# Counting sort of the edges: one-hots, histograms and lookups as engine loops of four groups instead of written out

## The reference

```python
h = x @ Wn.T + bn;  e = edge_attr @ We.T + be
a = leaky_relu(sum((h[src] + e) * attn), 0.01)
a = softmax of a over the edges that share dst
x = layernorm(x + relu(segment_sum(h[src] * a, dst)))      # first layer
agg = segment_sum(x[src'], dst');  cnt = segment_sum(1, dst')
x = layernorm(x + x @ W1.T + b1 + (agg / max(cnt, 1)) @ W2.T + b2)
```

## Time and profile before

| | |
|---|---|
| time before, median of 3 runs | 1555.24 us (1553.36 to 1556.54) |
| profiled execution | 1551.7 us, span of the core 1548.2 us |
| granted TensorE clock, mean | 0.904 |
| TensorE busy | 1198.5 us, 77% of the span |
| VectorE busy | 1067.6 us, 69% |
| ScalarE busy | 767.5 us, 50% |
| GpSimd busy | 746.3 us, 48% |

### The profile page before, as it was taken

One profiled execution on the slowest core, in us unless ns is written; L12 is line 12 of the kernel. 1 busy time (PEld: TensorE's weight loads), 2 busy tenths in 40 slices (PEclk: granted clock), 3 DMA queues, 4 the chain that ended last, 5 costly groups with the idle time before them and its releaser, 6 DMA issues.

```text
span 1548.2 us, 24971 instructions
## 1 busy us (share of the span) xinstructions
PE 1198.5 (77%) x6537; PEld 1030.5 (67%) x6537; DVE 1067.6 (69%) x4021; ACT 767.5 (50%) x1718; POOL 746.3 (48%) x731
## 2 busy tenths in 40 slices
PE   4567667627602999994999999998996888888884
PEld 3456556626501888883888888787785777777773
DVE  8855567515568555553999999998898666666661
ACT  5543357314300444442777777676775344434442
POOL 1066660466660677775444410555533345655563
PEclk9898889969955999997999999999999888888897
DMA  7744348647599666665666676888884123223321
GB/s 218 215 103 108 97 98 253 191 131 234 169 279 328 112 91 98 97 78 120 218 233 240 235 247 237 271 295 287 294 288 159 59 86 98 80 88 94 88 81 46
DMA packets 118445, 261.09 MB, mean 169 GB/s; under 512 B 23531, under 2 KB 57148, under 8 KB 118360
## 3 DMA queue, kind: packets, MB, share of 16 engines
q1 hardware_dynamic: 76026, 194.08, 39.5%
q0 software_dynamic: 40128, 64.45, 18.8%
q10 hardware_dynamic: 2206, 1.57, 0.3%
HBM read 182.48 MB, written 130.49 MB: 202 GB/s over the span
## 4 chain that ended last, share of the span: by engine, by line
PE 41%; DVE 22%; issue 12%; another core or an unknown queue 7%; ACT 6%; POOL 6%; DMA 5%; ACTq 0%; DVEq 0%; POOLq 0%
PE bank L1342 19%; DVE stats L929 9%; PE bank L1319 8%; DVE xin L762 4%; PE bank L1331 4%; POOL out_rows L478 3%; DMA xin<-z_scratch,idx_src 3%; PE bank L1383 3%; PE bank L1387 3%; PE bank L1264 3%; POOL xin L475 2%; ACT aggn L614 2%; DVE xT L765 2%; DVE X L762 2%
## 5 line engine op out<-in xcount | busy, mean ns | idle before, releaser
L1342 PE MATMUL bank<-w1T,xT 128*128 128x256 f32 x1968 | 480.6, 389 | 16.7 <-ACT yout L577 14.7
L1342 PEld LDWEIGHTS bank<-w1T,xT 128*128 128x128 f32 x1968 | 372.6, 195 | 79.6 <-ACT yout L577 15.7
L484 POOL DMA_INDIRECT order_scratch<-pay,rank_i x200 | 195.0, 975 | 239.5 <-DVE rank_i L857 97.7
L577 ACT ACTIVATE yout<-bank,nmr,rstd 128x256 f32<-128x256 f32 x492 | 251.9, 577 | 1.3 <-DVE nmr L765 1.3
L568 ACT COPY xT<-bank 128x512 f32<-128x512 f32 x296 | 174.1, 589 | 145.9 <-PE bank L1331 87.4
L929 DVE BATCH_NORM_STATS2 stats<-xin 128x6 f32<-128x512 f32 x246 | 159.1, 690 | 84.9 <-DMA xin<-z_scratch,idx_src 63.2
L929 DVE BATCH_NORM_STATS2 stats<-bank 128x6 f32<-128x512 f32 x246 | 166.5, 686 | 65.1 <-PE bank L1342 47.7
L1264 PE MATMUL bank<-X 128*128 128x196 bf16 x800 | 102.0, 267 | 132.5 <-ACT sel L662 65.1
L523 POOL DMA_INDIRECT z_scratch<-xin,idx_out x100 | 156.6, 1566 | 99.6 <-ACT xin L688 76.5
L765 DVE SCALAR_TENSOR_TENSOR bank<-iota_f,dig_f,bank 128x196 f32<-128x196 f32 x200 | 85.2, 426 | 152.3 <-PE bank L1319 77.7
L1264 PEld LDWEIGHTS bank<-X 128*128 128x128 bf16 x800 | 70.4, 105 | 166.8 <-ACT sel L662 77.0
(11 more groups left out here) (230 smaller groups left out, 1744.8 us busy)
## 6 DMA issues: line engine op xcount, KB each, us to landing
z_scratch<-in_x SPq DMA_DIRECT2D x125, 400.0 KB
xin<-z_scratch SPq DMA_DIRECT2D x97, 512.0 KB
out_rows<-yout SPq DMA_DIRECT2D x97, 512.0 KB
yout<-keys_scratch SPq DMA_DIRECT2D x50, 256.0 KB
kB<-sorted_scratch SPq DMA_DIRECT2D x50, 256.0 KB
yout<-low_digits_scratch SPq DMA_DIRECT2D x50, 128.0 KB
xin<-in_edge_attr SPq DMA_DIRECT2D x12, 512.0 KB, 5.4
order_scratch<-pay,rank_i POOLq DMA_INDIRECT x200
```

Of the source, the lines that this page charges most:

```text
L484: g.indirect_dma_start(out=order_dram[k], out_offset=bass.IndirectOffsetOnAxis(ap=rank_i[k][:, t:t + 1], axis=0), in_=pay[:, t, :], in_off ...
L577: a.activation(yout[hu][0:rows, j, :], bank_of(j // 2)[0:rows, (j % 2) * D:(j % 2 + 1) * D], ACT.Identity, bias=nmr[0:rows, slot, j:j + 1] ...
L1342: ins = mm(to, buf[:, jj, c, 0:n], w[:, c, :], start=not bias and i == 0 and c == 0, stop=i == len(terms) - 1 and c == 1)
```

## The change

The one-hots (`onehots`, `high_onehots`), the histogram (`count_group`), and the lookups (`tiles` on VectorE, `tables` on ScalarE, `look_up` on TensorE) go through `steps`. The first 4 groups and the last one stay written out and groups 4 to 23 go through a loop of four groups a pass (five passes); in the SRC lookups the first 8 stay, and groups 8 to 23 are looped (four passes). Inside a loop the tile number is a register: tiles of `onehot_lo`, `onehot_hi`, `dig_f`, `pay`, `earlier`, `found` and `rank_i` are addressed by it, and waits compare with a value in a register. SyncE's and GpSimd's programs are as they were.

```diff
+        def ring_at(k, m, u):
+            return (k * Q + u) % 4, m + (k * Q + u) // 4
+        def row_of(buf, t):
+            return buf[:, bass.ds(t, 1), :].rearrange("p a c -> p (a c)")
...
-                for q in range(Q):
-                    high_onehots(k, q)
+                steps(act, Q, 4, 4, 1, lambda q, m, u: high_onehots(k, q, u))
...
-                for i in range(T // 2):
-                    wait(act, s_add[k], 2 * i)
-                    wait(act, s_look[k], 2 * (i - 1))
-                    a.copy(table[i % 2].rearrange("p b c -> p (b c)"), bank[2][:, 0:2 * HC]).then_inc(s_tab, 1)
-                    if i % 2 == 0 and i // 2 + 1 < Q:
-                        upper_across(k, i // 2 + 1)
+                def tables(q, m, u):
+                    for half in range(2):
+                        wait(act, s_add[k], 4 * q + 2 * half)
+                        wait(act, s_look[k], 4 * q + 2 * half - 2)
+                        a.copy(table[half].rearrange("p b c -> p (b c)"), bank[2][:, 0:2 * HC]).then_inc(s_tab, 1)
+                        if half == 0 and in_range(q, 0, Q - 1):
+                            upper_across(k, q + 1, m, u + 1)
+                steps(act, Q, 4, 4 + 4 * k, 1, tables)
...
+                def group(q, m, u):
+                    for j in range(GT):
+                        t = q * GT + j
+                        ins = ts(row_of(onehot_lo, t), iota16[:], dig_f[k][:, 0, bass.ds(t, 1)], None, ALU.is_equal)
+                        if j % 2 == 0:
+                            ts(row_of(onehot_hi, t), iota16[:, 0:HC], dig_f[k][:, 1, bass.ds(t, 1)], None, ALU.is_equal)
+                    ins.then_inc(s_onehot, 1)
+                steps(dve, Q, 4, 4, 1, group)
...
-                ins = stt(pair_junk[odd], keys[:, (j - odd) * P:(j + 1) * P], pay[:, t:t + 1, k],
+                ins = stt(pair_junk[odd], keys[:, (j - odd) * P:(j + 1) * P], pay[:, bass.ds(t, 1), k],
-                                  accum_out=earlier[:, t:t + 1])
+                                  accum_out=earlier[:, bass.ds(t, 1)])
-                stt(o, iota_f[:, 0:HC], dig_f[k][:, 1, t:t + 1], o, ALU.is_equal, ALU.mult,
-                    accum_out=found[:, t:t + 1]).then_inc(s_found[k], 1)
+                stt(o, iota_f[:, 0:HC], dig_f[k][:, 1, bass.ds(t, 1)], o, ALU.is_equal, ALU.mult,
+                    accum_out=found[:, bass.ds(t, 1)]).then_inc(s_found[k], 1)
+                steps(dve, Q, 4, 8 if between else 4, 1, group)
...
-                    ins = mm(o[:, b * HC:(b + 1) * HC], onehot_lo[:, t, b * P:(b + 1) * P], onehot_hi[:, t, :],
+                    ins = mm(o[:, b * HC:(b + 1) * HC], row_of(onehot_lo[:, :, b * P:(b + 1) * P], t), row_of(onehot_hi, t),
...
+                def count_group(q, m, u):
+                    pe.wait_ge(s_onehot, k * Q + q + 1)
+                    pe.wait_ge(s_hotA, k * Q + q + 1)
+                    for j in range(GT):
+                        count_tile(hist, q * GT + j)
+                steps(pe, Q, 4, 4, 1, count_group)
...
+                def look_up(q, m, u):
+                    for half in range(2):
+                        pe.wait_ge(s_tab, k * T // 2 + 2 * q + half + 1)
+                        for j in (2 * half, 2 * half + 1):
+                            count_tile(tab, q * GT + j).then_inc(s_add[k], 1)
+                        if half == 0:
+                            pe.wait_ge(s_lbT, k * Q + q + 1)
+                            pe.wait_ge(s_lbA, k * Q + q + 1)
+                        for j in (2 * half, 2 * half + 1):
+                            wait(pe, s_found[k], q * GT + j - 3)
+                            for b in range(2):
+                                ins = mm(bank[3 + j][:, 0:HC], onehotT[(k * Q + u) % 2][:, b, j * P:(j + 1) * P],
+                                         table[half][:, b, :], start=b == 0, stop=b == 1)
+                            ins.then_inc(s_look[k], 1)
+                steps(pe, Q, 4, 4 + 4 * k, 1, look_up)
```

More of the change, by code:

```diff
@@ L619, in is_zero, with high_onehots, upper_across @@
                 return a.activation(o, gap_in, ACT.Relu, bias=ones[:, 0:1], scale=-1.0)
[L621 to L627, removed]
+            def high_onehots(k, q, u):
+                wait(act, s_hotA, k * Q + q - 1)
+                at = [(GT * q + j, gap_hi[2 * ((k * Q + u) % 2) + j // 2]) for j in (1, 3)]
+                for t, o in at:
+                    gap(o, iota16[:, 0:HC], -1.0, dig_f[k][:, 1, bass.ds(t, 1)])
+                for i, (t, o) in enumerate(at):
+                    ins = is_zero(row_of(onehot_hi, t), o, 3 * Q * k + 2 * q + 1 + i)
                 ins.then_inc(s_hotA, 1)
-            def upper_across(k, q):
-                n = k * Q + q
-                act.wait_ge(s_lb[n % 4], 16 * (n // 4 + 1))
+            def upper_across(k, q, m, u):
+                b, turn_no = ring_at(k, m, u)
+                act.wait_ge(s_lb[b], 16 * turn_no + 16)
                 wait(act, s_look[k], GT * (q - 1))
-                if k == SRC and q < 2:
+                if k == SRC and isinstance(q, int) and q < 2:
                     act.wait_ge(s_look[DST], T)
-                wait(act, s_lbA, n)
-                made = gap(gap_low, lowB[n % 4], -1.0, slot_f[:, 1:2])
-                is_zero(onehotT[n % 2][:, 1, :], gap_low, made).then_inc(s_lbA, 1)
+                wait(act, s_lbA, k * Q + q)
+                gap(gap_low, lowB[b], -1.0, slot_f[:, 1:2])
+                is_zero(onehotT[b % 2][:, 1, :], gap_low, 3 * Q * k + 2 * Q + q + 1).then_inc(s_lbA, 1)
             def dense_copy(h, h_par, p):
@@ L656, in _ @@
                     act.wait_ge(s_zero, 80)
[L657 removed]
+                upper_across(k, 0, 0, 0)
                 act.wait_ge(s_seed, k + 1)
[L659 to L665 removed]
+                def tables(q, m, u):
[5 more added lines that the diff above has]
+                            upper_across(k, q + 1, m, u + 1)
+                    if k == SRC and isinstance(q, int) and q == ORDER_AT + 2:
                         store_sorted(DST)
+                steps(act, Q, 4, 4 + 4 * k, 1, tables)
             act.wait_ge(s_expin, 1)
@@ L1304, in sort @@
                    skip_group_check=True).then_inc(s_seed, 1)
[L1306 to L1317, removed]
+                def look_up(q, m, u):
[8 more added lines that the diff above has]
+                            wait(pe, s_found[k], q * GT + j - 3)
                             for b in range(2):
-                                ins = mm(bank[3 + t % 4][:, 0:HC], onehotT[n % 2][:, b, j * P:(j + 1) * P], table[i % 2][:, b, :],
-                                         start=b == 0, stop=b == 1)
+                                ins = mm(bank[3 + j][:, 0:HC], onehotT[(k * Q + u) % 2][:, b, j * P:(j + 1) * P],
+                                         table[half][:, b, :], start=b == 0, stop=b == 1)
                             ins.then_inc(s_look[k], 1)
-                    if q in after:
+                    if isinstance(q, int) and q in after:
                         after[q]()
+                steps(pe, Q, 4, 4 + 4 * k, 1, look_up)
                 nothing(tab, start=False, stop=True)
```

61 lines of the change are left out of this document (24 added, 37 removed).

## The result

The kernel before now has the median 1554.3 us (four runs, 1551.87 to 1556.54), the changed one 1578.93 us (four runs, 1575.83 to 1580.27). The ratio is 1.0157, 95% interval 1.0127 to 1.0187: slower, by 24.6 us. The forecast was 1579 us. The profiled execution took 1578.96 us, 27.3 more than the one before, its span 1577.2 us, 29.0 more.

What follows compares the result with a forecast made beforehand. No engine is full; the lookups were taken as a cycle set by GpSimd's transfer floor and the others' catching up. 0 + 2 + 14.5 + 7.7 = 24 us on the median 1555.2 gives 1579 us; range 1528 to 1618 us.

Steps and rivals of the forecast that it cites:

- The cycle around GpSimd: Lookups: GpSimd's run of eight transfers delays the other engines' signals, they fall behind, GpSimd runs dry, they catch up.
- What the sorts lose is lost in full: Stages after the sorts follow in order, so any time lost in the sorts adds fully to the total.
- DST lookups, +14.5: Looped DST lookups: 1.45 us lost per two groups in short gaps and GpSimd's restart, x 10, 14.5 us.
- A slower pace breaks the cycle (faster): Rival, lookups: at about 5.2 us a group GpSimd pauses after each four transfers, no delay builds; -19 us, chance 0.10.
- SRC histogram, +2: TensorE's looped SRC histogram: one 0.1 us sequencer step a product, just hidden; between 0 and 12 us, 2 taken.
- The upper bound, two steps a product: TensorE's histogram: with two register steps a product a group needs about 2.0 us, 12 us over 20 looped groups.
- One operation an instruction: VectorE's looped one-hots: one register operation each, 0.13 us, hidden behind the instruction before; 0 us.
- DST histogram covered: DST sort: the histogram's added time hides in the 8.5 us its product waits for VectorE's edge features; 0 us.
- SRC lookups, +7.7: Looped SRC lookups: gathers wait for the count alone, without ranks; 1.1 us x 7, 7.7 us.
- Loop turn 0: All loops: a turn back costs nothing that reaches the array, read from the looped stage where TensorE is always busy.
- Late code: Rival, both sorts: TensorE's waits for "issue" are late instruction fetches that loops remove; -35 us, 1520 us, chance 0.14.
- the rival: Each loop turn waits for code: 11 turns on the path at 1.4 us, +15 on the forecast, 1594 us, chance 0.06.

Runs made afterwards that it cites:

- tensor_written: The changed kernel with all of TensorE's part written out again, VectorE's and ScalarE's still looped: 1579.12 us, 1.0084 times the kernel before on the same chip.
- the last four kernels: The kernel before with only TensorE's, VectorE's or ScalarE's lookups looped, or only one-hots and histograms (two groups a pass): 1.0095, 1.0008, 1.0025, 1.0086 times before.
- scatter_after_changed: The changed kernel with GpSimd's DST scatters held back until all DST ranks are made: 1636.40 us, one run.
- look_tensor_only: The kernel before with only TensorE's part of the lookups looped: 1437.49 us, 1.0095 times the kernel before on the same chip.

## Why the prediction was right, and where only by luck

The total is right to 0.1 us; that is luck in good part. Two terms miss by 7 us in opposite directions, and the profiles that the stages are read from differ by 29.0 us, 5 more than the sum of 24; the medians differ by 24.6, because the profiled execution before lies 2.6 us below its median.

- **The cycle around GpSimd** holds in its main point: with GpSimd held back the lookups take 95.0 us instead of 144.1. That the delay lies in how the engines "hear of each other" is not shown; fewer signals did not help. "What the sorts lose is lost in full" holds: the rest of the span changed by 1.8 us.
- **DST lookups, +14.5.** Measured +16.5, scatters' span 164.5 in the forecast's 160 to 166. But the working behind the size doesn't stand. The bare price is 0.57 us a looped group, not 1.1, and most of it TensorE's. Twenty groups at 0.57 are 11.3 of the 16.5 us. Beside the scatters even VectorE's and ScalarE's loops, bare 1.3 and 2.6 us, lengthen the stage by 12 us or more (tensor_written, 160.6 against 144.1 to 148.6). Hence no sum of per-group prices gives it; what enlarges them was not found.
- **"A slower pace breaks the cycle (faster)"** had its event right and its sign wrong. GpSimd's runs of eight did in part fall apart into fours, but the stage became longer: GpSimd paused 18 times instead of 12, and longer.
- **SRC histogram, +2** measured +9.5 between the copies and +12.9 from first to last product, where 0 to 3 was to be seen. This step failed in size: the prediction took one sequencer step of 0.1 us a product, just hidden. TensorE makes three register operations for two products (42 to 79 ns fused, 32 to 36 plain), and with their issue a tile of two products needs 0.37 us; with the waits a group needs 1.72 us, and the loop turn adds 0.40. The upper bound, two steps a product, gave 12, nearly what came. One operation an instruction was right for VectorE, whose one-hots stayed at 29.2 us; it was carried from there to TensorE.
- **DST histogram covered** holds, but only just: the product that needs the histogram had waited 8.5 us and now waits no more, and it comes at 67.6 us instead of 66.0. That the first copy is only 0.3 us later is luck with the clock. Before, TensorE had stood idle, and from 67.6 to 70.1 us it was granted 0.50; now it comes straight from the histogram and has 1.00, and the product that puts the table in its bank takes 0.93 us instead of 1.68.
- **SRC lookups, +7.7** measured +0.8, the gathers' span 145.8 where 147 to 153 stood. That the short gaps of a disturbed cycle show the price in full was wrong here. In both kernels these lookups nearly stand when GpSimd begins its gathers: groups 7 to 9 take 53.6 us before and 53.8 now, where the free pace gives 11.6, while GpSimd issues back to back. The 14 groups behind them, all looped now, take 84.9 us instead of 81.4, 0.25 us more a group, and 3.0 us of that is won back at the last copy. The copies are 3.0 us apart on average (2.9 before), not 2.3. On the chip without the disturbance TensorE's loop lengthens these lookups by 10.6 us (94.4 to 105.0), but GpSimd's gathers, slower than either pace, span 132.0 us there and hide it. Why the disturbed SRC lookups swallow most of the price and the DST ones enlarge it stays open.
- **Loop turn 0** was too low: in the histogram, where TensorE's sequencer sets the pace, five turns cost 5 x 0.40 = 2.0 us. The 0 was read in a stretch where TensorE is full.
- **Late code** is out: from 60 to 230 us TensorE fetched 2 blocks instead of 5 (60 to 220 us), and the DST lookups still became longer. The waits for "issue" did not vanish but grew, to 144.4 us before line 1274's weight loads; a loop's register operations count as such a wait too. The Trainium skill ("Runtime: NRT & Kernel Launch", section "Instruction fetch mechanics") has a taken branch stall when its target lies outside the two-page window. The loops here do not show that case: between 112.3 and 251.6 us, with the four turns back of the DST lookups, TensorE fetched nothing, and a turn of the histogram at 0.40 us is far from the 1.4 us that the rival gave it.

None of these versions beats both kernels. The nearest, the kernel before with one `s_add` a half group, is at 0.9982 (0.9961 to 1.0003), not told from no change.

## What to carry to other kernels

Before a loop replaces written-out code, count the dynamic addresses of the engine whose instructions are shortest: 0.1 us products on TensorE leave no room for three register operations for two, while 0.2 us instructions on VectorE hide one each. Read the price of a loop turn, and the time of a written-out group, in the stage that is to be looped: where the array is full a turn cannot be seen, and a group of 1.40 us in one histogram was 1.19 in the other. And in a cycle of four engines that runs behind GpSimd's transfers a per-group price says little about the total: hold one engine back, or take another chip, to see the bare price.

## What the runs showed of the hardware

**GpSimd's back-to-back indirect transfers slow how the other engines proceed, on some chips.** The written-out DST lookups take 144.1 us beside them and 95.0 without. On the chip of the last four kernels they take 93.2 beside them. The starkest case is the SRC sort of the kernel before: 38 gathers fall in the 53 us from 287 to 340, and the lookups advance by three groups. From the last SRC copy to the end it is 1112 to 1122 us on that chip and 1122 to 1124 in the two profiles above, and the two stages of lookups differ by 144.1 - 93.2 + 167.2 - 94.4 = 123.7 us: nearly all of the 130 us between the chips is here.

**The step of a sequencer itself can grow.** In scatter_after_changed the scatters run beside the looped SRC histogram, and from 225.7 us on in one unbroken row of 74. In that row TensorE's sequencer comes to this; one line of the kernel between 263 and 274 us:

```profile
L1274 PE MATMUL bank<-X x6: 324/324/324, 263.6 to 273.4; 128*128 x6
L1274 PEldq FUSED_REGOPS  x6: 700/700/700, 264.2 to 272.6; - x6
L1274 PEldq ALU_OP  x1: 700/700/700, 269.8 to 269.8; - x1
```

A register operation takes 700 ns where it took 46, and products start at multiples of 1.4 us. The stretch from the last DST copy to the first SRC one is 163.4 us. With written-out code it is 41.5, but that histogram is done 12 us before its unbroken row begins; in the first 32 us beside scatters the written-out histogram makes all its 200 products, the looped one 110. Single register operations of 0.7 us appear before the row is unbroken, from 188 us on, on VectorE and ScalarE too.

The changed kernel has such operations too, right behind the DST lookups: four of ScalarE's (641 to 720 ns) and five of VectorE's (678 to 782 ns) between 239.6 and 243.9 us, where TensorE waits 3.0 us for the one-hots; before it waited 2.0 there. In its DST lookups no register operation takes over 104 ns, so this state is not their loss. On the chip of the last four kernels it did not appear beside the lookups: 77 scatters in one row run beside TensorE's looped lookups in look_tensor_only, and none of its register operations there takes over 88 ns. What the engines contend for was not found.
